# A graph layer with a mixture of experts: what the expert table holds, and who adds x1 to the output

## The reference

```
xn  = layernorm(x)
x1  = x + gnn(xn, edges) + attention_with_gate(xn)
u   = layernorm(x1) * gamma + beta          # mean and variance over 256 features
lg  = u @ Wr + br                           # 8 experts
two largest of lg -> experts e0, e1; weights w = softmax of the two
out = x1 + sum over the two experts of w_e * ( gelu(u @ W1[e] + b1[e]) @ W2[e] + b2[e] )
```

## Time and profile before

| | us |
|---|---|
| median of 3 runs | 4450.23 (4450.19 to 4452.52) |
| the profiled execution | 4440.3 |
| its span, first to last instruction | 4438.6 |
| edge stage, POOL's first to last add | 157.5 to 3257 |
| routing stage | 3261 to about 3647 |
| expert stage | about 3647 to the end |

### The profile page before, as it was taken

One profiled execution on the slowest core, in us unless ns is written; L12 is line 12 of the kernel. 1 busy time (PEld: TensorE's weight loads), 2 busy tenths in 40 slices (PEclk: granted clock), 3 DMA queues, 4 the chain that ended last, 5 costly groups with the idle time before them and its releaser, 6 DMA issues. The chain is left out here.

```text
span 4438.6 us, 85552 instructions
## 1 busy us (share of the span) xinstructions
PE 3389.3 (76%) x16628; PEld 2802.7 (63%) x16629; DVE 2495.7 (56%) x11386; ACT 1685.6 (38%) x3095; POOL 3111.7 (70%) x2088
## 2 busy tenths in 40 slices
PE   1466666667677677878888888888758859999998
PEld 1355555555565555666666666666557758888887
DVE  3577777665555555666666666666548862222222
ACT  1233333344444443444444444444312224444443
POOL 0488888888888888888888888888855544444444
PEclk7788878788888888888888888888779979999999
DMA  9888888877777777777777777777789965565554
GB/s 380 241 146 155 152 148 147 157 117 118 116 109 115 116 113 114 102 108 108 105 104 107 108 103 105 108 107 102 91 217 296 294 187 143 139 145 141 141 140 114
DMA packets 588869, 638.95 MB, mean 144 GB/s; under 512 B 60524, under 2 KB 553156, under 8 KB 587138
## 3 DMA queue, kind: packets, MB, share of 16 engines
q0 software_dynamic: 279264, 269.84, 48.5%
q1 hardware_dynamic: 262234, 273.19, 20.9%
q10 hardware_dynamic: 47304, 95.18, 5.9%
HBM read 249.82 MB, written 390.09 MB: 144 GB/s over the span
## 5 line engine op out<-in xcount | busy, mean ns | idle before, releaser
L818 POOL DMA_INDIRECT agg<-msg,sidx x1664 | 2585.7, 1554 | 667.5 <-issue 408.7
L1122 PE MATMUL bank<-rows,Cmat 128*128 x3328 | 1025.7, 450 | 166.7 <-ACT msg L1315 140.6
L1315 ACT COPY msg<-bank 128x512 f32<-128x512 f32 x832 | 487.1, 585 | 1486.0 <-DMA agg<-msg,sidx 1209.8
L1122 PEld LDWEIGHTS bank<-rows,Cmat 128*128 128x128 f32 x3328 | 699.1, 224 | 346.7 <-issue 253.8
L873 DVE SCALAR_TENSOR_TENSOR sidx<-seen_sum,trash,srcf 128x4 int32<-128x4 f32 x416 | 92.7, 223 | 1022.8 <-DMA agg<-msg,sidx 1017.6
L2069 POOL DMA_INDIRECT out_dram<-x_y,x_node x210 | 325.7, 1551 | 473.1 <-issue 228.2
L856 DVE TENSOR_SCALAR Emat<-bank,srcf,wtf 128x128 f32<-128x128 f32 x1664 | 564.5, 398 | 0.0
L1106 PEld LDWEIGHTS bank<-Emat,pick 128*128 128x128 f32 x3328 | 518.3, 226 | 41.6 <-issue 17.7
L1106 PE MATMUL bank<-Emat,pick 128*128 128x128 f32 x3328 | 528.7, 311 | 1.6 <-DVE seen L860 1.6
L1097 PE MATMUL bank<-packed,both 128*128 (+1 forms) x416 | 187.3, 451 | 437.9 <-DVE seen L860 427.9
L860 DVE SCALAR_TENSOR_TENSOR seen<-bank,srcf,prior 128x128 f32<-128x128 f32 x1664 | 479.1, 341 | 0.0
(11 more groups left out here) (245 smaller groups left out, 4130.6 us busy)
## 6 DMA issues: line engine op xcount, KB each, us to landing
x_w<-in_L_ffn_W_dram SPq DMA_DIRECT2D x105, 512.0 KB, 4.1
agg<-expert_rows ACTq DMA_DIRECT2D x12, 4224.0 KB, 63.3
r_agg<-agg SPq DMA_DIRECT2D x196, 256.0 KB
x_zin<-table SPq DMA_DIRECT2D x105, 259.0 KB, 4.1
window_raw<-in_x_dram SPq DMA_DIRECT2D x208, 128.0 KB, 2.5
agg<-msg,sidx POOLq DMA_INDIRECT x1664
xn_rows<-n_xn ACTq DMA_DIRECT2D x49, 256.0 KB
xn_turned<-n_xnT ACTq DMA_DIRECT2D x49, 256.0 KB
```

The source lines that it names most:

```text
L818: pool.indirect_dma_start(scratch["agg"][r][:, :], bass.IndirectOffsetOnAxis(ap=sidx[:, j:j + 1], axis=0), msg[:, j % (2 * BATCH), :], Non ...
L1122: mm = nc.tensor.matmul(M[p][:, (q % 2) * D:(q % 2 + 1) * D], Cmat[:, b % 2, q, :], rows[:, bass.ds(slot, 1), :], start=True, stop=True)
L1315: nc.scalar.copy(msg[:, at:at + 2, :].rearrange("p q c -> p (q c)"), M[p][:, :]).then_inc(s_msg, 1)
```

## The change

The expert table in HBM gets rows of 261 numbers in place of 259: x1 itself, the node, the first choice, the lead, the mean and the scale (one over the deviation).

In routing, `gather_sums` writes x1 straight into the four-slot buffer `row`, from which the sends go, and now it waits for the sends of pair i-4. The normalising operations are gone; the scale goes into the row. PE turns x1 as it is, ACT copies it, and PE multiplies by a centred Wr times gamma, prepared once; DVE multiplies the product by the scale and adds a prepared bias. SP stores no x1 to the output.

In the expert stage four row slots are loaded three blocks ahead. DVE normalises the rows of the next block into `x_normal`, makes a mask of the rows whose first choice is the block's expert, multiplies x1 by it into `x_residual`, and adds that in the last operation. So the scatter-add brings x1 to the output once, with the first choice.

In the edge stage ACT writes zeros to the output, 512 KB in each of the first 25 groups, at place 8 (the last one is shorter), from a part of the zeroed buffer; SP waits for these before it loads W2 of expert 7 over it.

```diff
 # edge_phase, SP
             context_turn(DOUBLES - 1)
+            sp.wait_ge(s_blankout, 16 * DOUBLES)
             load_expert(7)
 # edge_phase, ACT
+            def blank_out(n):
...
+                    act.dma_start(out[bass.ds(n * BLANK * P, BLANK * P), :].rearrange("(p a) d -> p (a d)", a=BLANK),
+                                  blank).then_inc(s_blankout, 16)
-                steps = [(1, lambda u=u: deviations(n, u)) for u in pairs_of(n)]
+                steps = [(1, lambda u=u: deviations(n, u)) for u in pairs_of(n)] + [(8, lambda: blank_out(n))]
 # route_phase, SP
-                sp.wait_ge(s_sum, i + 1)
-                sp.nop(nofuse=True)
...
-                    sp.dma_start(pair_of(out, i), x1[:, u % 2]).then_inc(s_x1st[u % 2], 16)
                 if more:
+                    sp.wait_ge(s_sum, i + 1)
+                    sp.nop(nofuse=True)
                     load_x(i + DEPTH, u)
 # route_phase, DVE
+            for a in range(HALF):
+                nc.vector.tensor_scalar(wrg[:, a, :], wrt[:, a, :], gamma[:, a:a + 1], None, ALU.mult)
+                last = nc.vector.tensor_scalar(wrb[:, a, :], wrt[:, a, :], beta[:, a:a + 1], None, ALU.mult)
...
             def gather_sums(i, u):
-                x = x1[:, u % 2]
                 dve.wait_ge(s_ld[u], 16 * visits(i, u) + 16)
                 if not below(i, 2):
-                    dve.wait_ge(s_z, i - 1)
-                    dve.wait_ge(s_x1st[u % 2], 16 * ((i - u % 2) // 2))
+                    dve.wait_ge(s_T, i - 1)
+                if not below(i, DEPTH):
+                    for c in range(2):
+                        for m in range(2):
+                            dve.wait_ge(s_sent[c][m], 16 * (i - DEPTH + 1))
                 dve.wait_ge(s_rest, i + 1)
+                nc.vector.tensor_tensor(row[:, u, :, 0:D], xin[:, u], REST[u % 2][:, :].rearrange("p (c d) -> p c d", c=2),
+                                        ALU.add).then_inc(s_sum, 1)
-            def normalise(i, u):
+            def scale(i, u):
                 s = u % 2
                 dve.wait_ge(s_std, i + 1)
+                nc.vector.reciprocal(row[:, u, :, RSTD], std[:, s]).then_inc(s_scl, 1)
+                nc.vector.tensor_copy(row[:, u, :, NODE], nodes[:, bass.ds(2 * i, 2)])
...
-                for c in range(2):
-                    last = nc.vector.tensor_scalar(z[:, u, c, 0:D], x1[:, s, c, :], mv[:, s, c, 0:1], scl[:, s, c:c + 1],
-                                                   ALU.subtract, ALU.mult)
 # route_phase, PE: turn
-                pe.wait_ge(s_z, i + 1)
+                pe.wait_ge(s_sum, i + 1)
 # expert_phase, SP
+                if not over(q + AHEAD):
+                    if not below(q, 1):
+                        sp.wait_ge(s_xe, q)
+                        sp.nop(nofuse=True)
+                    load_rows(*ahead(k, u, AHEAD))
 # expert_phase, DVE
+            def normalise(k, u):
+                q, s = SLOTS * k + u, u % 2
+                dve.wait_ge(s_row[u], 16 * k + 16)
+                if not below(q, 2):
+                    dve.wait_ge(s_T, q - 1)
+                for c in range(2):
+                    last = nc.vector.tensor_scalar(zn[:, s, c, :], row[:, u, c, 0:D], row[:, u, c, MEAN:MEAN + 1],
+                                                   row[:, u, c, RSTD:RSTD + 1], ALU.subtract, ALU.mult)
+                last.then_inc(s_zn, 1)
...
+                nc.vector.tensor_scalar(own[:, s], row[:, u, :, FIRST], iota8[:, bass.ds(e, 1)], None, ALU.is_equal)
...
+                for c in range(2):
+                    last = nc.vector.tensor_scalar(xe[:, s, c, :], row[:, u, c, 0:D], own[:, s, c:c + 1], None, ALU.mult)
+                last.then_inc(s_xe, 1)
...
-                    nc.vector.tensor_scalar(y[:, s, c, :], y[:, s, c, :], share[:, s, c:c + 1], None,
-                                            ALU.mult).then_inc(s_y, 1)
+                    nc.vector.scalar_tensor_tensor(out=y[:, s, c, :], in0=y[:, s, c, :], scalar=share[:, s, c:c + 1],
+                                                   in1=xe[:, s, c, :], op0=ALU.mult, op1=ALU.add).then_inc(s_y, 1)
+            def body(k, u):
+                q = SLOTS * k + u
+                if not over(q + 1):
+                    normalise(*ahead(k, u, 1))
+                shares(k, u)
+                finish(k, u)
```

More of the change, by code:

```diff
@@ L1457, in below, with route_phase @@
     return isinstance(i, int) and i < n
-def route_phase(nc, scratch, out, psum, ident, ones, iota8, lower, run, nodes, ffn, iotaq, base, offset, expert):
+def route_phase(nc, scratch, psum, ident, ones, iota8, lower, run, nodes, ffn, iotaq, base, offset, expert):
     with ExitStack() as ctx:
@@ L1764, in _ @@
             pe.wait_ge(s_bits, 1)
+            pe.wait_ge(s_wr, 1)
+            for n, w in enumerate((wrg, wrb)):
+                for a in range(HALF):
+                    mm = nc.tensor.matmul(psum[2][:, n * NE:(n + 1) * NE], ones[:], w[:, a, :], start=(a == 0), stop=(a == HALF - 1))
+            mm.then_inc(s_wrs, 1)
             def sum_turned(i, u):
@@ L1869, in features @@
                     act.wait_ge(s_L, i - 1)
-                for a in range(HALF):
-                    last = nc.scalar.activation(xf[:, s, a, :], T[s][:, a * D:(a + 1) * D], ACT.Identity,
-                                                bias=beta[:, a:a + 1], scale=gamma[:, a:a + 1])
-                last.then_inc(s_xf, 1)
+                nc.scalar.copy(xf[:, s].rearrange("p a c -> p (a c)"), T[s][:, :]).then_inc(s_xf, 1)
             sum_out(0, 0)
@@ L1981, in body @@
                     mm.then_inc(s_H, 1)
-                if not (isinstance(k, int) and q == BLOCKS - 1):
-                    turn(*((k, 1) if s == 0 else (k + 1, 0)))
-                if not first(k):
+                if not over(q + 1):
+                    turn(q + 1, 1 - s)
+                if not below(q, 2):
                     pe.wait_ge(s_yb, q - 1)
```

210 lines of the change are left out of this document (115 added, 95 removed).

## The result

| | before | after |
|---|---|---|
| median of the runs taken together, us | 4451.05 (4450.19 to 4452.52, 4 runs) | 4596.78 (4591.12 to 4604.21, 4 runs) |
| the profiled execution, us | 4440.3 | 4597.8 |
| its span, us | 4438.6 | 4596.1 |

What follows compares the result with a forecast made beforehand. No engine full overall: POOL paced the edge stage, DVE's order routing, PE the expert stage. Routing 0 - 2, expert start +2, edge +1 gave +1 on the 4450.23 median: 4451 us, range 4423 to 4472.

Steps and rivals of the forecast that it cites:

- Rows are loaded three blocks ahead, behind less critical waits: Expert stage, SP's row loads: the earlier loading was taken to add no delay, priced at 0.
- The mask and the products (1.1 us more) lie in DVE's idle time: Expert stage, DVE: this work fits into over 4 us of idle time before the next output product, costing nothing.
- Rival (c): Expert stage: DVE's operations lengthen each of POOL's two sends by 0.2 us, scatter-add becomes the bound; +30 us, 4481; chance 0.08.
- The forecast's closing sentence: Routing stage: the prediction fails above all if sends' landing time depends on order of loads and sends more than traffic.
- The descriptor rule: POOL's sends: DVE's two-port operations block descriptor writing; by the rule 4481 us, by one trace row of 0.96 us, 4451.
- The ring: Routing: a sum waits for sends of four pairs back, so two turns take at least 10.04 us plus landing; turn 7.2.
- L: Routing: time from a send's issue end until the waiting engine goes on; bounded 1.7 to 5.4 us, taken as 4.3.
- term of 10.04 us: Routing, two turns without the landing: 0.86 + 3.78 + 0.96 for the sends and 4.44 from sum to positions.
- DVE's own pace would be 6.4 us: Routing, DVE's work per pair: 7.0 less 1.0 for removed operations plus 0.4 for new ones and waits.
- The wait ahead of the sum: Routing, sign of the forecast: DVE idle there until the table rows' DMA releases it, 0.6 to 0.9 us a pair.
- (d): Edge stage: zeroing the output stalls POOL's adds, up to +17 us instead of +1, 4467 us; chance 0.07.
- the signs given for (c): Expert stage, profile after: PE has gaps before its products and POOL's starts lie over 7.35 us apart.

Runs made afterwards that it cites:

- rows two ahead: The changed kernel with expert rows loaded two blocks ahead instead of three, into the same four slots; 4466.5 us, ratio 1.0043 to the kernel before.

## Why the prediction was wrong

**The step that failed** is the one sentence of the expert stage: "Rows are loaded three blocks ahead, behind less critical waits." The wait is for the residual product, the product comes behind the node numbers, and those wait for adds to land [after, 4099.74]. I listed what the wait was for, and not what is queued behind the row load on SP: the next W1 load. It was priced at 0 and cost 130 us in the traces; "rows two ahead" gave all of it back. With it fell the step before it, "The mask and the products (1.1 us more) lie in DVE's idle time": they do, as DVE's work, but the product had become a signal, and the time from the landing to that signal was on the ring.

**Rival (c)** named the right place, the cycle of the scatter-add, and even the warning (7.57 us between sends where PE needs 7.35), with a chance of 0.08. The 7.57 was one interval; the mean was 7.35, with no slack behind it. Its mechanism was the wrong one. It made the sends longer by 0.2 each; they grew by 0.11 in the mean. It took the landing as a constant, and that was the term: 1.11 of 1.32 us. The forecast's closing sentence, that it would fail if landing "depends on the order of loads and sends more than on the amount of traffic", came true in the stage where it had not been applied. The Trainium skill (page "DMA: Bandwidth & Descriptors", section "Queues, rings and completion order") says that each DMA engine takes turns between its queues packet by packet; the trace agrees so far as adds and loads begin in the same microseconds, and the second add crawls while 403 KB of loads begin beside it in two microseconds (121 KB in the two in which both adds went before). No row here shows the order of the packets on one engine.

**The descriptor rule** (the Trainium skill, page "SBUF — State Buffer", section "SBUF: two separate sides") says that a VectorE operation in a two-port mode locks GpSimd out of the port by which it writes its DMAs' descriptors. The forecast held that the trace disagreed for this shape, by one row of 0.96 us. That is one row, and it does not show in which mode the operation ran. The expert stage shows an effect, a second send of 1.73 us where `x_normal` runs beside it and 1.55 where it does not (rows two ahead, medians), and none of the size that a blocked engine would give: eight operations beside the first sends lengthened these by 0.06 us and the time by nothing. The effect is real and small for these operations. No run shows whether any of them ran in a two-port mode, so the rule itself is neither borne out nor refuted here.

**Routing.** The ring was right and mis-sized, and the price of 0 against it came from the choice of L. Its term of 10.04 us (sum to the end of the last send) measured 10.86 in the mean: 4.81 from sum to positions instead of 4.44, with waits for the ranks in it, and 6.05 to the end of the fourth send instead of 5.60. The 5.60 was one pair's; some sends take up to 2 us, in the kernel before too, whose mean was 5.94. L, taken as 4.3, had a median of 4.5 where the sum waited; that it was so near is luck, for 4.3 was read from no row but is the L with which the ring equals the old turn. (10.86 + 4.5) / 2 = 7.7 is the ring, and 7.65 was the period in the loaded stretch of 3300 to 3580 us, for a forecast of 7.2. Over all 48 pairs it was 7.47 against 7.01 to 7.35 before, so some 14 us for 0. "DVE's own pace would be 6.4 us" is refuted as a saving that could be had: without the wait for the sends the period was 7.35 and 7.53, and 0.57 us of idle work put back cost nothing.

**What held.** The wait ahead of the sum, released by the table's DMA, was there: 28.4 us in 36 pairs, 0.79 a pair, forecast 0.6 to 0.9. The edge stage cost nothing that shows, for a forecast of 1: routing's first load starts between 3259 and 3262 us in five traces of the old code and, but for one at 3257, in eleven of the new one. POOL's rate is unchanged; (d) is excluded. The preparation of the router weights, costed at nothing with "about 3 us once" if uncovered, and the start of the expert stage, costed at 2, cost about 1 us each in the means of these traces, which is within their spread. PE had gaps ahead of its products and POOL's starts lay over 7.35 apart, the signs given for (c).

**What stays open.** Why routing needs 7.35 to 7.7 us a pair in every form of the change, and why the kernel before needs 7.01 in one execution and 7.35 in another. None of the wait for the sends, the loop's edge, PE's order of ranks, VectorE's work and the store is the sole cause, and the granted clock is not shown to be one. What remains is the exchange between DVE and PE (ranks, logits, halves' sum), in which PE sometimes stands without a recorded reason; no run shows that it is the cause. No form beat the kernel before: the best, 4461.1 and 4463.4, are still 0.24% slower.

## What to carry to other kernels

When a wait is added on a queue, write down what is queued behind it, and follow the signal back to its first release. Here a load waited for a product, the product for node numbers and these for a landing, and the next 512 KB load stood behind. A DMA's landing time is no constant of the kernel; in a loop where one landing releases the next load, where the load falls among the next sends decides the cycle, and 1 or 2 us of delay in an engine with idle time can put it there. When a stage has two cycles of almost equal length (PE's products and the adds, both 7.35 here), price both with their terms as variables before calling anything hidden. And read a stage's length from more than one execution: here one code had 336 to 353 us for the same 48 pairs.

## What the runs showed of the hardware

The same 770 KB of loads for each block delayed the second add by next to nothing when most of them went ahead of both adds (the first landed 4.09 us behind its send, the second 2.97; without W1's 512 KB the second took 2.88) and cost 1.1 us a block when they ran beside the second (2.83 and 4.12). In the kernel before, whose loop body has four pairs, most periods in the loop are 6.9 to 7.0 us and the one at its edge is 7.8. A straight run of code did not end the long periods in the changed kernel: with eight pairs in a loop body VectorE waited up to 5.4 us at the edge for nothing shown (15.0 us in three places of 280), and written out, other periods of 9 to 12 us came, in some of which PE stood for 3 us. And DMA engines 0.95 busy over a whole stage hardly bound it: without the store they were 0.85 busy, the period was 7.04 us where the same code with it had 7.01 to 7.35, and the time was 0.14% less.
